# A DLRM tower with a compressed interaction network: dense products and id transposes placed in the second chunk instead of the first, and an earlier release of its gathers

## The reference

```python
e = jnp.stack([tbl_0[ids[:, 0]], ..., tbl_38[ids[:, 38]]], axis=1)   # 512 x 39 x 16
x1 = einsum('bid,bjd,ijh->bhd', e, e, W0.reshape(39, 39, 128))
x2 = einsum('bid,bjd,ijh->bhd', e, x1, W1.reshape(39, 128, 128))
z = sum(concatenate([x1, x2], axis=1), axis=-1)                      # 512 x 256
h = concatenate([z, dense_ctx], axis=1)                              # 512 x 272
h = maximum(h @ W_top1 + b_top1, 0)
h = maximum(h @ W_top2 + b_top2, 0)
y = h @ W_top3
```

## Time and profile before

| what | value |
|---|---|
| runs | 233.32, 233.53, 234.63 us; median 233.53 |
| profiled execution | 233.34 us, of which the span (first to last instruction) 231.4 us |
| granted TensorE clock, mean | 0.985 |
| instructions | 4819 |
| chain that ended last | PE 78%, DVE 5%, DMA 4%, issue 4%, POOL 3%, ACT 3% |
| DMA | 8.57 MB, two queues; gathers 0.78 MB |

### The profile page before, as it was taken

How to read it: one execution, slowest core, us unless ns; L and a number is a source line. 1 busy time by engine, 2 the same in 40 slices (tenths; PEclk the granted TensorE clock), 3 DMA queues, 4 the chain that set the end, 5 groups by cost and what they waited for, 6 DMA issues and landing times.

```text
span 231.4 us, 4819 instructions
## 1 busy us (share of the span) xinstructions
PE 215.8 (93%) x1717; PEld 172.2 (74%) x1717; DVE 164.3 (71%) x347; ACT 160.0 (69%) x319; POOL 98.6 (43%) x99
## 2 busy tenths in 40 slices
PE   4489799997889999999999999999999999999996
PEld 4378367674566578988787788887876788887995
DVE  3989988967598996977869996866587855561101
ACT  3996889797769786598685957787668585663201
POOL 4774377777557787750667777600000000000000
PEclk9979999999799999999999999999999999999999
DMA  4991009914000000000000000000000000000000
GB/s 122 243 305 21 3 11 284 260 13 94 6 7 7 7 9 6 10 6 0 9 5 7 9 7 9 6 1 3 0 0 4 0 0 3 0 0 3 0 0 3
DMA packets 7579, 8.57 MB, mean 37 GB/s; under 512 B 2631, under 2 KB 5164, under 8 KB 7556
## 3 DMA queue, kind: packets, MB, share of 16 engines
q1 hardware_dynamic: 4516, 7.48, 11.9%
q0 software_dynamic: 3040, 0.78, 3.5%
HBM read 8.25 MB, written 0.00 MB: 36 GB/s over the span
## 4 chain that ended last, share of the span: by engine, by line
PE 78%; DVE 5%; DMA 4%; issue 4%; POOL 3%; ACT 3%; SPq 1%; DVEq 0%; ACTq 0%
PE turn_bank L607 16%; PE x_bank L536 9%; PE pair_bank L508 8%; PE x_bank L539 8%; PE x_bank L538 8%; PE g_bank L570 5%; POOL emb L478 3%; PE misc_bank L570 3%; PE g_bank L587 3%; PE turn_bank L645 3%; PE x_bank L550 3%; DMA emb<-tbl,ids_sb 2%; PE turn_bank L618 2%; DMA tab<-small 2%; PE pair_bank L735 1%
## 5 line engine op out<-in xcount | busy, mean ns | idle before, releaser
L478 POOL DMA_INDIRECT emb<-tbl,ids_sb x95 | 98.4, 1035 | 50.5 <-ACT prod L1047 22.0
L1047 ACT ACTIVATE prod<-pair_bank 128x512 f32<-128x512 f32 (+1 forms) x108 | 64.6, 605 | 38.7 <-PE pair_bank L508 38.7
L897 DVE TENSOR_TENSOR prod_lo<-prod,prod_hi 128x512 fp32r<-128x512 f32 x92 | 61.6, 684 | 9.7 <-ACT prod_hi L1052 8.8
L536 PE MATMUL x_bank<-prod_hi,pair_w_hi 128*128 128x512 f32 (+1 forms) x108 | 60.5, 560 | 1.7 <-DVE prod_lo L897 1.0
L508 PE MATMUL pair_bank<-x,sel 117*128 117x512 bf16 (+1 forms) x112 | 42.2, 386 | 2.2 <-ACT prod L1047 1.4
L607 PEld LDWEIGHTS turn_bank<-g_sb,w_sb 128*128 128x128 f32 x312 | 40.0, 191 | 3.4 <-issue 1.0
L607 PE MATMUL turn_bank<-g_sb,w_sb 128*128 128x128 f32 x312 | 42.3, 278 | 0.0
L1052 ACT ACTIVATE prod_hi<-prod 128x512 fp32r<-128x512 f32 x64 | 40.8, 638 | 0.2
L538 PE MATMUL x_bank<-prod_lo,pair_w_hi 128*128 128x512 f32 x92 | 36.9, 401 | 0.0
L539 PE MATMUL x_bank<-prod_hi,pair_w_lo 128*128 128x512 f32 x92 | 36.9, 401 | 0.0
L885 DVE CAST prod_hi<-prod 128x512 fp32r<-128x512 f32 x44 | 18.5, 421 | 16.5 <-ACT prod L1047 16.4
(11 more groups left out here) (147 smaller groups left out, 304.0 us busy)
## 6 DMA issues: line engine op xcount, KB each, us to landing
emb<-tbl,ids_sb POOLq DMA_INDIRECT x95, 2.4
tab<-small SPq DMA_DIRECT2D x2, 560.0 KB
wt<-w_top SPq DMA_DIRECT2D x2, 512.0 KB
tab<-small SPq DMA_DIRECT2D x1, 504.0 KB
wa<-pair_w_a SPq DMA_DIRECT2D x1, 448.0 KB
wb<-pair_w_b SPq DMA_DIRECT2D x1, 448.0 KB
wtd<-w_dense SPq DMA_DIRECT2D x1, 256.0 KB
dense_sb<-dense_t SPq DMA_DIRECT2D x1, 256.0 KB
```

The costliest lines, as they stand in the source:

```text
L478: pool.indirect_dma_start(out=emb[:, at:at + D], out_offset=None, in_=tables[f], in_offset=bass.IndirectOffsetOnAxis(ap=ids_sb[:, c * M + ...
L536: mm = pe.matmul(x1_banks[k % 2][:, :], pair_w_hi[p, t, :], hi(n), start=(t == 0), stop=(t == FULL))
L897: dve.tensor_tensor(lo(n), prod[rows, n % RING, :], prod_hi[rows, n % RING2, :], ALU.subtract).then_inc(lo_done, 1)
L1047: act.activation(prod[0:ROWS[t], n % RING, :], pair_bank[n % 2][0:ROWS[t], :], ACT.Square).then_inc(sq_done, 1)
```

## The change

Five edits:

1. `LATE_AT` becomes (30, 34, 38): the last three groups of id transposes, with ACT's copies one step later, go to chunk 1.
2. The four dense products go to steps 28, 32, 36 and 40. All use `turn_bank`, DVE copies all four one step later, and products and id transposes wait in turn for the bank to be read out. ACT's two dense copies and the semaphore `dense_act` are gone.
3. POOL starts chunk 1's gathers when all splits of chunk 0 are done, and no longer when the turned rows are copied.
4. The first later look-up (chunk 1, part 0) stands in step 5 instead of 4, which puts its five one-hots in steps 0, 0, 1, 2, 3 instead of 0, 0, 0, 1, 2.
5. SP loads `idf`, `wtd` and `dense_sb` in this order behind its wait for chunk 0's gathers.

```diff
-LATE_AT = (NT + 1, 2 * NT + 3, 2 * NT + 5)
+LATE_AT = tuple(NB * NT + n for n in (2, 6, 10))
+
+DENSE_AT = tuple(NB * NT + n for n in (0, 4, 8, 12))
...
-        dense_bank = [g_bank[0], g_bank[1], x1_banks[1], turn_bank]
...
-            return ((c - 1) * NB + part + (c > 1 and PARTS[c] < 3)) * NT + LOOK_AT
+            return ((c - 1) * NB + part + (c > 1 and PARTS[c] < 3)) * NT + LOOK_AT + (nth(c, part) == 0)
...
+            sp.wait_ge(gathered[0][0], gathers(0))
+            sp.dma_start(idf[:, :], ident_f).then_inc(idf_in, 16)
             sp.dma_start(wtd[:, :], w_dense).then_inc(dense_in, 16)
             sp.dma_start(dense_sb[:, :], dense_t).then_inc(dense_in, 16)
-            sp.wait_ge(gathered[0][0], gathers(0))
-            sp.dma_start(idf[:, :], ident_f).then_inc(idf_in, 16)
...
                 if c == 1:
-                    pool.wait_ge(x3_a, 2)
-                    pool.wait_ge(x3_b, 1)
+                    pool.wait_ge(split_done, pieces(0))
...
             def layer2(c, i0, i1):
                 if i0 == 0:
                     pe.wait_ge(g_act, 2 * NB * (c + 1))
                     pe.wait_ge(g_dve, 2 * NB * (c + 1))
+                    pe.wait_ge(dense_dve, M1)
...
             def dense_part(m):
-                pe.matmul(dense_bank[m][:, 0:B - CH], wtd[:, m * 128:(m + 1) * 128], dense_sb[:, 0:B - CH], start=True,
+                if m == 0:
+                    pe.wait_ge(dense_in, 32)
+                wait(pe, dense_dve, m)
+                wait(pe, later_ids_ok, HEAD_SLOTS // 8 + sum(at < DENSE_AT[m] for at in LATE_AT))
+                pe.matmul(turn_bank[:, 0:B - CH], wtd[:, m * 128:(m + 1) * 128], dense_sb[:, 0:B - CH], start=True,
                           stop=True).then_inc(dense_mm, 1)
...
+                if n in DENSE_AT:
+                    dense_part(DENSE_AT.index(n))
                 if n in LATE_AT:
-                    pe.wait_ge(dense_act, 2)
+                    wait(pe, dense_dve, sum(at < n for at in DENSE_AT))
                     pe.wait_ge(later_ids_ok, HEAD_SLOTS // 8 + LATE_AT.index(n))
...
-            pe.wait_ge(dense_in, 32)
-            dense_part(0)
-            dense_part(1)
             for part in range(len(TURNS)):
                 turn(0, part)
             step(0)
             step(1)
             pe.wait_ge(pair_w_done, 1)
-            dense_part(2)
             step(2)
-            dense_part(3)
             step(3)
...
+                if n - 1 in DENSE_AT:
+                    keep_dense(DENSE_AT.index(n - 1))
                 for part in hot_at(n):
                     later_one_hot(*part)
...
-            keep_dense(0)
             keep_turned(0)
...
-            keep_dense(1)
             for n in range(NB * NT):
                 step(n)
```

More of the change, by code:

```diff
@@ L216, in build_tower @@
         dense_dve = sem("dense_dve")
-        dense_act = sem("dense_act")
         h1_sum = sem("h1_sum")
@@ L532, in layer1 @@
                     wait(pe, g_dve, 2 * (k - 1))
-                    if k == 1:
-                        pe.wait_ge(dense_act, 2)
                 p = slice(0, ROWS[t])
@@ L553, in contract_d @@
             def contract_d(k, pair):
-                if k == 0 and pair == 0:
-                    pe.wait_ge(dense_dve, 2)
                 if pair == 0:
@@ L925, in relu1 @@
                     return
-                dve.wait_ge(dense_act, 2)
-                dve.wait_ge(dense_dve, 2)
+                dve.wait_ge(dense_dve, M1)
                 dve.wait_ge(h1_mm, M1 * (c + 1))
@@ L968, in keep_dense @@
                 dve.wait_ge(dense_mm, m + 1)
-                dve.tensor_copy(dense_h1[:, m, :], dense_bank[m][:, 0:B - CH]).then_inc(dense_dve, 1)
+                dve.tensor_copy(dense_h1[:, m, :], turn_bank[:, 0:B - CH]).then_inc(dense_dve, 1)
             halve_ids()
@@ L1137, in step @@
                     keep_turned(c + 1)
-            def keep_dense(m):
-                act.wait_ge(dense_mm, m + 1)
-                act.activation(dense_h1[:, m, :], dense_bank[m][:, 0:B - CH], ACT.Copy).then_inc(dense_act, 1)
             def keep_table(n):
@@ L1184, in _ @@
             keep_turned(0)
[L1185 to L1190, removed]
+            for n in range(NB * NT):
                 step(n)
```

## The result

The changed kernel takes 239.14 us (median of 4 runs, 238.84 to 239.21), the kernel before in the same comparison 234.08 (233.32 to 236.12). The ratio is 1.019, 95% interval [1.015, 1.023]: slower by 5 us where 1.8 was forecast, and outside the range, which ended at 237.1. The profiled execution took 238.84 us with a span of 236.9, so 5.5 us more span than in the profile before.

What follows compares the result with a forecast made beforehand. TensorE was taken as the bound from chunk 1 on, with slack at chunk 0's end, which the gathers set. Term 1 (-1.94) and term 2 (+3.75) summed to +1.8 us, forecast 235.3 us, range 233.5 to 237.1.

Steps and rivals of the forecast that it cites:

- term 1: Chunk 1's gathers: released earlier, they bring chunk 1's first transposes forward, -1.94 us (bounds 0 to -4.3).
- term 2: Chunk 1 up to layer 2: the moved dense products and id transposes cost +3.75 us (bounds 2.8 to 4.8).
- What bounds: TensorE has about 4.6 us of slack at chunk 0's end, set by the gathers, and nearly none in early chunk 1.
- All 27 move by 1.94: Chunk 1's gathers on GpSimd: all start 1.94 us earlier, and the splits and chunk 1's first transposes move with them.
- The prologue: Ahead of chunk 0: its first product can come 0.8 to 0.9 us earlier, but this is hidden, worth 0.
- Hidden: 0: Work that comes sooner ahead of the gathers' gate gains 0, as GpSimd sets that gate.
- Rival 2: Start of chunk 1: a longer TensorE idle gap puts the half clock there, costing 1.7 us, 236.9 us; chance 0.20.
- dense 1: Second dense product, step 32: TensorE waits 1.0 us for ScalarE's id copy, bringing the lag to 2.45 to 2.5 us.
- The unit price: TensorE time of one dense product, two fp32 matmuls of 384 columns: 0.67 us each, four 2.7 us.
- the walk: Chunk 1 stepped through the in-order queues with old times, the lag growing to 3.75 us at layer 2's first products.
- dense 2: Third dense product, step 36: no wait for the bank, 0.67 us more, lag 3.0 us.
- rival 4: Chunk 1's gathers: squares or a weight transfer hold them, so term 1 is 0, 237.3 us; chance 0.03.

Runs made afterwards that it cites:

- c_gap: The changed kernel with the id transposes back in chunk 0 (steps 8, 17, 19) and the four dense products in steps 23 to 26: 233.40 us.
- d_two: The kernel before with the earlier gather release and dense products 2 and 3 moved to steps 24 and 26, 0 and 1 left in place: 232.79 us.
- b_look: The kernel before with only the first look-up one step later and its one-hots in steps 0, 0, 1, 2, 3: 236.84 us.
- a_ids_back: The changed kernel with the id transposes and their copies back in chunk 0 (steps 8, 17, 19), dense products still in chunk 1: 236.32 us.
- a_psum: The changed kernel with one operand of VectorE's chunk 0 low parts taken from PSUM, plus one matmul to fill that bank: 234.80 us.
- a_warm: The changed kernel with twelve filler matmuls in TensorE's gap at the end of chunk 0: 237.59 us.
- b_look_warm: b_look with the twelve filler matmuls of a_warm and the waits for turn_bank they need: 234.51 us.
- b_moved: The kernel before with only the dense products and late id transposes moved to chunk 1: 238.61 us.
- b_release: The kernel before with only the earlier release of chunk 1's gathers: 233.52 us.

## Why the prediction was wrong

Direction and the main cost were right; the size was not, and the range missed. The span grew by 5.5 us where 1.8 was forecast. Of the 3.6 between, term 1 makes 1.8, the clock behind A 1.4 and term 2 0.4.

- *What bounds.* TensorE's slack ahead of A and the lack of it in chunk 1 were read rightly: the earlier trace rows and B to C show it, and c_gap and d_two live on it.
- *Term 1, -1.94 us*: the step that failed. "All 27 move by 1.94" took each gather's duration along to its new place, on the ground that what runs beside the slowest one stays in the kernel. The runs show that a gather's duration is set by where its start falls in VectorE's order: move the queue, and other gathers are stretched. Measured: -0.13. The prediction had the one long gather in view, 1.64 us beside VectorE's subtraction, and used it only to keep the pace as it was; it should have priced term 1 from it, as each of 27 starts drawing 0 to 0.7 us anew. "All 27" also took GpSimd's issue alone for what holds them. The third gather's margin of 2.2 us was also spent, by the move of 1.94 and a first square 0.6 later.
- *The prologue*, priced 0: its first square came 0.6 later, by the stretched gather at 15.86, and chunk 0's first product stands at 29.35, 0.1 sooner and not 0.8 to 0.9. The clock fell there too, as foreseen (0.52 from 26.0 to 29.35 and 0.50 from there to 32.0); whether that cost anything at A no run separates. That the first gather came at the forecast time is two errors that cancel (0.49 and 0.51).
- *"Hidden: 0" for what comes sooner in chunk 0*: the second step that failed. The gap ahead of A grew from 1.37 to 3.17 us, and the clock fell behind it. Rival 2 had this, with "full clock where it was halved from 59.1 to 62.5", and a price of 1.7; it measured 1.42. The forecast counted the slack only as cover, but it is also where the clock is lost (b_look alone pays 2.2 us from A to B).
- *Term 2, +3.75*: measured 4.16. The wait at dense 1 was forecast at 1.0 and is 1.04. The unit price was right: 2.64 for four in a_ids_back, 2.77 in the changed kernel, 2.68 forecast.
- *Term 2 by parts.* In the walk the ids and their wait are the rest, 3.75 - 2.68 = 1.07; they measured 1.52, and this is the missing 0.4. By the lags it arose at dense 1 and dense 2; what made it there no run separates. The 2.4 of the expectation for a_ids_back was a worse price than the walk's: it added up work and wait and left out the waits that the ids had filled.
- *The range.* It took rivals 2 and 4 as exclusive. Term 1 at 0 lengthens nothing by itself, but both go back to the gathers' gate, and together they give 233.5 + 3.75 + 1.7 = 239.

Shown by runs: the gathers' stretch (a_psum), the clock's price (a_warm, b_look_warm), the move's cost (b_moved), the release's worth in the kernel before (b_release). The edits run alone give +3.8 (b_moved), -1.3 (b_release) and +2.1 us (b_look), +4.6 in sum beside the 5.1 of the medians, so the look-up's new step may well be what opens the gap in the changed kernel. That is only argued: neither it nor the release was taken out of the changed kernel alone, and the order of the loads was never run by itself. Only argued too is that the changed kernel's four runs all drew a late gate because of the later first square.

## What to carry to other kernels

Work moved out of a stretch that waits for a transfer buys nothing there and can cost twice: it is paid in full where it lands (2.64 us for the four products in chunk 1), and a longer gap can lower TensorE's clock for what follows (0.51 from A to B behind 4.30 us of idle time in b_look, 0.63 behind 3.17 in the changed kernel). In the gap such work is free as far as it fits (two products here). Price a move of gathers by what VectorE runs at their starts, not by the durations of the old places, and quote it with the spread that this gives. When several cases of a forecast hang on one gate, add them up for the range's end.

## What the runs showed of the hardware

An indirect DMA of 128 rows takes GpSimd 0.94 us, but one that starts inside a VectorE instruction with all operands in SBUF takes 0.94 + the rest of that instruction - 0.12 us, up to 1.83 here. In the twelve traces 389 gathers start more than 0.09 us into such an instruction with over 0.18 us left, and 387 take this sum within 0.03 us. For 138 of them the instruction is a cast or a one-hot comparison, with a single tensor as its input. Of 208 that start so inside an instruction with an operand in PSUM, 203 take 0.94 to 0.98 (as at 60.62).

Starts that nearly coincide go either way. Of 35 gathers that start in the first 0.04 us of a subtraction of two SBUF tiles, 17 are stretched, and 18 are not; there VectorE's instruction is some 0.03 to 0.07 us longer (0.73 at 35.11). A subtraction that starts more than 0.2 us into a gather of at most 0.98 us is not held: 137 of them took 0.68 to 0.69 us.
